# Sums of squares in two rounded parts, bounds read earlier, and a first gather without its index copy

## The reference, cut to what matters

```
q = _rmsnorm(layernorm(x) @ Wq.T  per head)      # 32 heads of 16
k = _rmsnorm((context @ Wk.T) per head)          # t * rsqrt(mean(t*t) + 1e-6)
attn = softmax(q k^T * 16**-0.5);  x = x + attn @ v
xt = layernorm(x)
gate = xt @ Wr + br;  ids = top_k(gate + gate_bias, 2);  probs = softmax over the two
out = sum over the two experts of probs * ffn_e(xt) + ffn_shared(xt)
ffn(t): u = t@Wup+bup;  g = silu(u@Wgate+bgate)*u;  g@Wdown+bdown
x = x + out
```

## Time and profile before

| | |
|---|---|
| median of 3 runs | 966.19 us |
| the profiled execution | 966.36 us |
| its span in the profile | 964.6 us |
| PE busy | 944.2 us, 98% |
| DVE busy | 706.1 us, 73% |
| ACT busy | 497.4 us, 52% |
| POOL busy | 208.1 us, 22% |
| granted TensorE clock, mean | 0.996 of full speed |

### The profile page before, as it was taken

One profiled execution on the slowest core, in us unless ns is written; L12 is line 12 of the kernel. 1 busy time (PEld: TensorE's weight loads), 2 busy tenths in 40 slices (PEclk: granted clock), 3 DMA queues, 4 the chain that ended last, 5 costly groups with the idle time before them and its releaser, 6 DMA issues.

```text
span 964.6 us, 17835 instructions
## 1 busy us (share of the span) xinstructions
PE 944.2 (98%) x6676; PEld 681.4 (71%) x6676; DVE 706.1 (73%) x1459; ACT 497.4 (52%) x619; POOL 208.1 (22%) x225
## 2 busy tenths in 40 slices
PE   8999999999999999999999999999999999999995
PEld 7634444454444454345989999999999999999995
DVE  7798767886678757885978886865867686758654
ACT  4588668866787658887234313323424244324221
POOL 1011000311012200320300001423323323333331
PEclk9999999999999999999999999999999999999998
DMA  9400100100201110313523104834535536625422
GB/s 334 170 1 23 66 1 1 45 33 24 76 2 44 45 66 1 110 56 130 203 74 112 67 23 142 235 73 71 180 67 146 117 71 204 197 48 166 115 49 39
DMA packets 32512, 87.42 MB, mean 91 GB/s; under 512 B 7744, under 2 KB 7744, under 8 KB 28352
## 3 DMA queue, kind: packets, MB, share of 16 engines
q1 hardware_dynamic: 21920, 60.70, 17.9%
q0 software_dynamic: 10528, 25.87, 12.9%
HBM read 61.83 MB, written 24.72 MB: 90 GB/s over the span
## 4 chain that ended last, share of the span: by engine, by line
PE 87%; DVE 6%; issue 2%; ACT 2%; DMA 1%; DVEq 0%; POOLq 0%; POOL 0%; SPq 0%; ACTq 0%
PE z_ps L907 16%; PE y_ps L907 15%; PE u_ps L907 15%; PE o_ps L642 11%; PE scores L626 8%; PE bank_a L679 5%; PE bank_b L663 5%; PE bank_b L649 2%; PE xt_ps L921 2%; PE bank_a L649 2%; PE tr L708 1%; PE tr L702 1%; PE tr L697 1%; DMA ctx_raw<-ctx_t 1%; ACT probs L1180 1%
## 5 line engine op out<-in xcount | busy, mean ns | idle before, releaser
L1180 ACT ACTIVATE probs<-scores 128x2048 f32<-128x2048 f32 x128 | 240.5, 1879 | 64.1 <-PE scores L626 61.1
L907 PE MATMUL z_ps<-u_hi,w_sb 128*128 128x256 f32 x896 | 167.6, 285 | 0.8 <-DVE u_lo L1869 0.8
L907 PE MATMUL u_ps<-x_hi,w_sb 128*128 128x256 f32 x864 | 159.2, 283 | 0.0
L1210 ACT ACTIVATE u_hi<-u_ps,b_ug 128x256 fp32r<-128x256 f32 x108 | 45.3, 471 | 198.8 <-PE u_ps L907 198.8
L907 PEld LDWEIGHTS z_ps<-u_hi,w_sb 128*128 128x128 f32 x896 | 140.6, 190 | 2.1 <-DVE u_lo L1869 1.2
L907 PE MATMUL y_ps<-w_sb,g_hi 128*128 128x512 f32 x448 | 139.8, 393 | 0.2 <-DVE g_lo L1887 0.2
L907 PEld LDWEIGHTS u_ps<-x_hi,w_sb 128*128 128x128 f32 x864 | 135.7, 190 | 1.1
L642 PE MATMUL o_ps<-probs,v_sb 128*17 128x512 f32 x1024 | 134.7, 598 | 0.0
L907 PE MATMUL z_ps<-u_lo,w_sb 128*128 128x256 f32 x448 | 126.5, 282 | 0.0
L907 PE MATMUL u_ps<-x_lo,w_sb 128*128 128x256 f32 x432 | 122.2, 283 | 0.0
L1222 ACT ACTIVATE s_sb<-z_ps,b_ug 128x256 f32<-128x256 f32 x112 | 47.0, 471 | 99.6 <-PE z_ps L907 99.6
(11 more groups left out here) (247 smaller groups left out, 1594.9 us busy)
## 6 DMA issues: line engine op xcount, KB each, us to landing
w_raw<-w_all SPq DMA_DIRECT2D x27, 1024.0 KB, 6.9
ctx_raw<-ctx_t SPq DMA_DIRECT2D x4, 1024.0 KB, 6.8
out<-x_sb SPq DMA_DIRECT2D x16, 256.0 KB, 2.0
xg<-xt_dram POOLq DMA_DIRECT2D x14, 256.0 KB, 3.4
x_sb<-x SPq DMA_DIRECT2D x1, 3072.0 KB, 17.4
xn<-x_t SPq DMA_DIRECT2D x12, 256.0 KB, 4.4
xn_dram<-xn SPq DMA_DIRECT2D x12, 256.0 KB, 2.1
xt_dram<-xt SPq DMA_DIRECT2D x6, 512.0 KB, 3.0
```

The source lines that it names most:

```text
L907: ins = nc.tensor.matmul(out_ps, stat[a], mov[b], start=(first and a + b == 0), stop=(last and a == 1), skip_group_check=True)
L1180: nc.scalar.activation(probs[:, t % 2], scores[:], ACT.Exp).then_inc(p_ready, 1)
L1210: last = nc.scalar.activation(u_hi[:, c, :], u_ps[:, b, a, :], ACT.Identity, bias=b_ug[:, par, 0, c:c + 1])
```

## The change

What it does, part by part:

- **Sums in two parts.** For 20 of the 32 sums (`HALVED`: `sum_q` of units 2 to 15, and `sum_k` of units 3, 4, 7, 8, 11 and 12, whose step also holds a value tile) GpSimd copies `sq` to `sq_hi` in FP32R, VectorE subtracts it into `sq_lo`, and TensorE multiplies each part by an FP32R copy of `blocks`, two matmuls in place of one FP32 one. The next square waits for `sq_low` in place of `tr_ready`.
- **Turns.** `K_TURNS` gives step 7 two turns in place of one, step 0 three in place of four.
- **`q_st`** has one buffer for both parities of the unit; `stack_q` waits until the scores that read it are done.
- **Bounds.** VectorE reads bounds 1 and 2 in tile 4, 3 and 4 in tile 5, 5 and 6 in tile 6, 7 in tile 7, each in `during_z`.
- **Gather.** The first gather takes its rows from `table` itself, with no copy to `index`, and GpSimd's own read of the bounds stands ahead of it.
- **Start.** TensorE's first matmul waits for the FP32R copy of `blocks` as well (128 x 128 on GpSimd).

```diff
-        q_st = asb("q_st", [P, 2, 2, SEQ], FP32R)
+        q_st = asb("q_st", [P, 2, SEQ], FP32R)
+        sq_hi, sq_lo = asb("sq_hi", [P, SEQ], FP32R), asb("sq_lo", [P, SEQ], FP32R)
+        blocks_r = asb("blocks_r", [P, P], FP32R)
+        SUMS = [("sum_k", 0), ("sum_q", 0), ("sum_q", 1)]
+        HALVED = {}
+        for u in range(UNITS):
+            _, g, more, _ = batch_of(u)
+            if u + 1 < UNITS:
+                SUMS.append(("sum_k", u + 1))
+                if more and g >= 2:
+                    HALVED[SUMS[-1]] = len(HALVED)
+            if u + 2 < UNITS:
+                SUMS.append(("sum_q", u + 2))
+                HALVED[SUMS[-1]] = len(HALVED)
-        K_TURNS = {6: (0, 4), 7: (4, 5), 0: (5, 9), 1: (9, 12)}
+        K_TURNS = {6: (0, 4), 7: (4, 6), 0: (6, 9), 1: (9, 12)}
...
+            def squares_high(use):
+                pool.wait_ge(sqk_done if use[0] == "sum_k" else sqq_done, use[1] + 1)
+                for other, n in HALVED.items():
+                    if n == HALVED[use] - 1:
+                        pool.wait_ge(tr_ready, TR_AT[other] + 1)
+                nc.gpsimd.tensor_copy(sq_hi[:], sq[:]).then_inc(sq_high, 1)
...
                     root2_q(u + 1)
+                    if ("sum_k", u + 1) in HALVED:
+                        squares_high(("sum_k", u + 1))
                     root2_k(u + 1)
...
                     norm2(b - 1, 2)
+                if u + 2 < UNITS:
+                    squares_high(("sum_q", u + 2))
+                if behind and g == 2:
                     norm2(b - 1, 3)
...
-                first = isinstance(n, int) and n == NA
-                if first:
+                if isinstance(n, int) and n == NA:
                     pool.wait_ge(xl_done, n * 2)
+                    pool.wait_ge(dense_stored, 16)
                     pool.wait_ge(table_ready, 1)
-                    pool.wait_ge(dense_stored, 16)
+                    picked_rows = table[:, 2:4]
                 else:
...
-            gather(NA)
             pool.wait_ge(start_ready, 1)
             total = bound(pool, ER)
+            gather(NA)
             gather(NA + 1)
...
+            def sum_halves():
+                nc.tensor.matmul(tr[:], blocks_r[:], sq_hi[:], start=True, stop=False)
+                nc.tensor.matmul(tr[:], blocks_r[:], sq_lo[:], start=False, stop=True).then_inc(tr_ready, 1)
             def sum_q(u):
                 begin("tr", TR_AT, ("sum_q", u), tr_free)
-                pe.wait_ge(sqq_done, u + 1)
-                nc.tensor.matmul(tr[:], blocks[:], sq[:], start=True, stop=True).then_inc(tr_ready, 1)
+                if ("sum_q", u) in HALVED:
+                    pe.wait_ge(sq_low, HALVED["sum_q", u] + 1)
+                    sum_halves()
+                else:
...
-            pe.wait_ge(blocks_set, 3)
+            pe.wait_ge(blocks_set, 4)
...
+            def squares_low(use):
+                dve.wait_ge(sq_high, HALVED[use] + 1)
+                nc.vector.tensor_tensor(sq_lo[:], sq[:], sq_hi[:].bitcast(FP32), ALU.subtract).then_inc(sq_low, 1)
...
+            def half_scored(u, ab):
+                if u:
+                    dve.wait_ge(sc_ready, STEPS * (u - 1) + MT * (ab + 1))
...
                     if more and g == 2:
                         context_split(b + 1, 1)
+                    if ("sum_k", u + 1) in HALVED:
+                        squares_low(("sum_k", u + 1))
...
                     if nxt:
                         stack_k(u + 1, 0)
+                    if u + 2 < UNITS:
+                        squares_low(("sum_q", u + 2))
...
-            tile(4, 0, x_tile=8, during_u=positions, during_y=lambda: hot_rows(0))
-            tile(5, 0, x_tile=10, during_u=lambda: hot_cols(0),
+            tile(4, 0, x_tile=8, during_u=positions, during_z=lambda: bounds(1, 3), during_y=lambda: hot_rows(0))
+            tile(5, 0, x_tile=10, during_u=lambda: hot_cols(0), during_z=lambda: bounds(3, 5),
...
-            tile(7, 0, x_tile=14, during_u=last_split, during_y=bounds)
+            tile(7, 0, x_tile=14, during_u=last_split, during_z=lambda: bounds(7, ER + 1))
```

More of the change, by code:

```diff
@@ L406, in gather @@
                     pool.wait_ge(row_saved, n - NA)
-                nc.gpsimd.tensor_copy(index[:], table[:, bass.ds((n - NA + 1) * 2, 2)]).then_inc(index_ready, 1)
-                pool.wait_ge(index_ready, n - NA + 1)
-                pool.sem_inc(passed)
+                    nc.gpsimd.tensor_copy(index[:], table[:, bass.ds((n - NA + 1) * 2, 2)]).then_inc(index_ready, 1)
+                    pool.wait_ge(index_ready, n - NA)
+                    pool.sem_inc(passed)
+                    picked_rows = index
                 for h in range(2):
@@ L412, in gather @@
                         out=xg[:, h, :], out_offset=None, in_=xn_dram,
-                        in_offset=bass.IndirectOffsetOnAxis(ap=index[:, h:h + 1].bitcast(mybir.dt.uint32), axis=0),
+                        in_offset=bass.IndirectOffsetOnAxis(ap=picked_rows[:, h:h + 1].bitcast(mybir.dt.uint32), axis=0),
                         ).then_inc(xg_loaded, 16)
@@ L626, in scored @@
                         last = nc.tensor.matmul(scores[:, j, :], part[rows, u % 2, ab, mt * P:(mt + 1) * P],
-                                                q_st[rows, u % 2, ab, :], start=(part is k_hi), stop=(part is k_lo),
+                                                q_st[rows, ab, :], start=(part is k_hi), stop=(part is k_lo),
                                                 skip_group_check=True)
@@ L1033, in x_high, with squares_taken @@
                 nc.scalar.activation(xt_hi[:, c, :], xn[:, c % 2 if b else c, :], ACT.Copy).then_inc(xt_high, 1)
+            def squares_taken(use):
+                ahead = SUMS[SUMS.index(use) - 1]
+                if ahead in HALVED:
+                    act.wait_ge(sq_low, HALVED[ahead] + 1)
+                else:
+                    act.wait_ge(tr_ready, TR_AT[ahead] + 1)
             def square_q(u):
                 act.wait_ge(b_ready, B_AT["q", u] + 1)
-                act.wait_ge(tr_ready, TR_AT["sum_k", max(u - 1, 0)] + 1 if u != 1 else TR_AT["sum_q", 0] + 1)
+                squares_taken(("sum_q", u))
                 nc.scalar.activation(sq[:], bank_b[:], ACT.Square).then_inc(sqq_done, 1)
@@ L1042, in square_k @@
                 if u:
-                    act.wait_ge(tr_ready, TR_AT["sum_q", u] + 1)
+                    squares_taken(("sum_k", u))
                 nc.scalar.activation(sq[:], bank_a[:], ACT.Square).then_inc(sqk_done, 1)
@@ L1427, in stack_q @@
                 done(nc.vector.stream_shuffle(twin[:], qn[:], (UPPER_TWICE, LOWER_TWICE)[ab]))
-                at = q_st[:, u % 2, ab, :]
+                at = q_st[:, ab, :]
+                half_scored(u, ab)
                 done(nc.vector.tensor_copy(at, twin[:]))
@@ L1935, in _, with bounds @@
             tile(3, 0, x_tile=6, before_x=totals_out, during_z=probabilities, during_y=steps_of(prefixes_out, starts))
-            tile(4, 0, x_tile=8, during_u=positions, during_y=lambda: hot_rows(0))
-            tile(5, 0, x_tile=10, during_u=lambda: hot_cols(0),
+            start_at = [0]
+            def bounds(first, end):
+                dve.wait_ge(start_ready, 1)
+                for e in range(first, end):
+                    start_at.append(bound(dve, e))
+            tile(4, 0, x_tile=8, during_u=positions, during_z=lambda: bounds(1, 3), during_y=lambda: hot_rows(0))
+            tile(5, 0, x_tile=10, during_u=lambda: hot_cols(0), during_z=lambda: bounds(3, 5),
                  during_y=steps_of(lambda: table_out(0), lambda: hot_rows(1)))
@@ L1943, in last_split @@
                 split(1, 1, 2)
-            tile(6, 0, x_tile=12, during_u=lambda: hot_cols(1),
+            tile(6, 0, x_tile=12, during_u=lambda: hot_cols(1), during_z=lambda: bounds(5, 7),
                  during_y=steps_of(lambda: table_out(1), splits(1, 1, [1])))
[L1947 to L1952, removed]
-            tile(7, 0, x_tile=14, during_u=last_split, during_y=bounds)
+            tile(7, 0, x_tile=14, during_u=last_split, during_z=lambda: bounds(7, ER + 1))
             def head(j, par, nth):
```

13 lines of the change are left out of this document (11 added, 2 removed).

## The result

The change made the kernel slower: 969.84 us (median of 7 runs, 969.07 to 972.02) against 966.37 us before (7 runs, 966.05 to 966.72). The ratio is 1.0037, with a 95% interval of 1.0026 to 1.0048. Predicted was 963.7. The profiled execution took 969.99 us, with a span of 968.2.

The account below looks back on a forecast made before the run. TensorE bounds most steps, above a floor of 2.72 us, with VectorE second in one place. Attention -0.9 and experts -1.6 gave -2.5, hence 963.7 us; own range 962.6 to 964.9, over all cases 961.5 to 966.0.

Parts of the forecast that it names:

- The late sums: Query sums in units 0, 1, 5 and 9: TensorE waits for VectorE's late `sq_lo`; together +3.6 us.
- group 2: Its 3 key sums: TensorE's sum is not what comes last, the new subtraction fits before `v_sb`; 0.
- the long steps: Units 6 and 10, before a long step: next S0 far from the floor, all of 0.39 counts; -0.8 us.
- the plain units: Units 2, 3, 4, 7, 8, 11, 12 and 13: S7, S0 and S1 shorten, -0.31 a unit; -2.5 us in all.
- group 3: Its 3 key sums: VectorE is idle there, `sq_lo` is ready in time, all of 0.39 counts; -1.2 us.
- contention rival: GpSimd's casts slow VectorE, in the four late units +1.2 to +2.5: 964.9 to 966.2 us; chance 0.11.
- S0: Step 0 of a unit, scores' start to next scores' start; in plain units 2.78 to 2.72 us, -0.06.
- S1: Step 1 of a unit, held by its exponential; in plain units 3.08 to 2.99 us, 0.09 taken.
- S7: Step 7 of a unit, from its scores to the next; in plain units 2.93 to 2.77 us, -0.16.
- Experts: First gather's DMA starts earlier, -0.87; bounds moved away from the chain ahead of tile 8's z product, -0.72; together -1.6 us.
- slow-cast rival: GpSimd's casts are slow and query sums wait for them; at 3.1 us a cast +4.3, 968.0 us; chance 0.05.
- rival of late sums that cost nothing: VectorE has `sq_lo` in time in units 0, 1, 5 and 9; 3.6 becomes a gain, 958.9 us; chance 0.07.

Follow-up runs that it names:

- e1: The changed kernel with the query sums of step 7 in units 0, 1, 5 and 9 left whole; 962.41 us.
- e4: The changed kernel with the subtraction `sq_lo` put ahead of `stack_k` in VectorE's step 6 of units 0, 1, 5 and 9; 963.37 us.
- e5: The changed kernel with eight extra FP32 matmuls ahead of TensorE's wait for `sq_lo` in units 0, 1, 5 and 9; 968.24 us.
- e10: Against e9, group 2's three key sums split again, GpSimd's cast of them held until `qn` has read the bank, S0 keeping its turn there; 960.20 us.
- e6: The kernel of e1 with the three key sums of group 2 whole as well, 13 split sums left; 961.69 us.
- e7: The kernel of e1 with GpSimd's cast of group 2's key squares held until VectorE (`qn`) has read the value tile's bank; 962.22 us.
- e8: The kernel of e6 with the key projection turn that the change moved from S0 to S7 put back in S0; 961.27 us.
- e2: The kernel before with only the experts' part: first gather from the table, seven bounds read in tiles 4 to 7; 964.69 us.
- e3: The kernel before with only the attention's part: 20 split sums, one `q_st`, the turns of the key projection; 971.57 us.
- e9: The kernel of e8 with the key projection turn moved to S7 only in units 2, 3, 4, 8, 12 and 13; 960.23 us.

## Why the prediction was wrong, point by point

*The late sums: the step that failed.* The prediction put +3.6 on units 0, 1, 5 and 9. The mechanism, the places and the queue behind the wait were as it said; e1 and e4 show both the cause and its place in the list. Their size was +8.6. Without the fall of the clock (e5) the four come to +1.0, +1.4, +1.55 and +1.5, together 5.4, so 3.2 is the clock. Of the 6.1 between the forecast and the measured time 5.0 are these four; 0.8 is group 2, 0.5 the long steps, 0.3 the plain units and 0.1 group 3, and some 0.6 goes the other way (the end of the kernel above all).

- *What the idle time did to the clock* had no term at all (+3.2). The forecast priced a wait by its length. Waits of 1.8 and 1.7 us cost 1.6 us more behind them, in the two of the four places where the clock fell.
- *The wait itself* was 0.5 longer in unit 5. `sq_lo` started 0.39 later than forecast, by the VectorE cast that GpSimd's cast stretched, and the sum started 0.15 behind its end, where I had put them together. Unit 0, forecast at one VectorE pitch of 0.65, cost 1.0, and unit 1, forecast at 0.9 to 1.0 from the pattern of unit 5, cost 1.4. Together +1.8.

Of the clock the Trainium skill (TensorE: Matmul & The Clock Gate, Part 1: The HAM clock gate) says that the throttled state is the default and activity releases it. e5 agrees: matmuls that nobody reads kept 1.00 where idling led to 0.50.

*The contention rival was right in part, at another place.* I gave it 0.11, looked at the late units alone, and held against it that the cast is over before `k_lo` starts. It was, and it hit the instruction ahead of that. Worse, it hit group 2. There the prediction had weighed what lies behind the value tile (`v_sb`, `ssk`) and found a cost of 0; e10 confirms that sum for units 6 and 10 and has 0.15 in unit 2. It had not looked at what stands ahead of the tile: `qn` with 0.08 of slack. In e1 these three units are 0.9, 0.6 and 0.7 longer than before, of which the moved turn is 0.8 in all (e6).

The Trainium skill (GPSIMD Engine Reference, Key points) names VectorE instructions with two SBUF inputs as exposed to GpSimd. `ctx_lo` in e1 agrees, 1.15 beside the cast and 0.69 in e7 without it; VectorE's plain cast with one input took 0.83 instead of 0.42 as well.

*Plain units: -2.2 for -2.5.* S0 at 2.72 and S1 at 2.98 were right. S7 is 2.82 and not 2.77, since the floor of that step is 2.82 (e8), and unit 13, where GpSimd normalizes late, has 2.99.

*Before a long step: -0.3 for -0.8.* The step "far from the floor, so all of 0.39 counts" failed. In S7 it counts when the turn is not moved there (3.48 to 3.09 in e8). The next S0 is held by VectorE's `gate`, so the turn that left it gave nothing back.

*Key sums of group 3: -1.1 for -1.2. Experts: -1.6 for -1.6* (e2), with `sq_lo` in time and the gather's DMA 1.2 earlier. Both right. The DMA's dispatch, taken as 0.7 from no row, was 0.89: the table ends at 580.92 and the DMA starts at 581.81; the slack behind it covered that.

*The slow-cast rival* falls: 20 casts have a mean of 0.68. *The rival of late sums that cost nothing* falls for this kernel. It would have needed another order on VectorE, and by e4 even that leaves unit 0 at +0.9.

What stays open is why the clock fell behind the idle of units 5 and 9, in both traces with these waits (after and e3), and not behind that of units 0 and 1. The idle times in the trace after are 1.79 and 1.72 in units 5 and 9, 1.77 and 1.52 in units 0 and 1, so the length doesn't separate unit 0 from them. The DMA traffic before and in the idle time (122 to 260 GB/s in units 5 and 9, 91 to 171 in unit 1, none in unit 0) doesn't separate them clearly either. GpSimd is busy for 3.9 to 4.0 of the 4 us from 184 and from 294, ahead of the idle time of units 5 and 9, and for 1.0 and 0.0 in the like stretches of units 0 and 1 (54 to 58, 78 to 82). No run separates these.

## What to carry to other kernels

Before a wait is put on the engine that bounds the kernel, read the slack of the producer at each place where the pattern occurs, from what stands ahead of it in its list, and split or move work only where it is there: the same split brought some 4.5 us in 13 places, with one turn moved in six units (e9 less the experts' 1.6), and lost 5.3 in 20 (e3). Price idle time of TensorE by more than its length, since the clock may fall behind it. And an instruction on a helper engine costs what it does to its neighbour at that moment, even when its own duration lies off the path: look for the producer with no slack next to it.

## What the runs showed of the hardware that was not expected

- Idle times of TensorE of 1.79 and 1.72 us were followed by 1.2 GHz for about 3.4 us, while one of 1.77 and one of 1.52 in the same run were not. Over the seven runs the mean granted clock and the time go together: 0.994 to 0.995 in the five at 969.07 to 969.99, 0.993 with 970.26, 0.991 with 972.02. In the five runs of e3 it is less strict: 0.998 with 969.76 and 0.992 with 972.40, but 0.995 with 970.93 and 0.996 with 971.76.
- GpSimd casts 128 x 512 from FP32 to FP32R in 0.61 to 1.00 us, mean 0.68, where its product of that shape takes 1.18. VectorE's instruction beside it grew by up to 0.46 (`ctx_lo`, 0.69 to 1.15; `xt_hi`, 0.42 to 0.83; `k_hi`, 0.49 to 0.64), and some did not grow (`qn`, 0.68 beside a cast).
- Adding eight matmuls to each of four waits made the kernel 1.6 us faster.
